# Two matmuls on a zero tile left out of each group of four recurrence steps, in a transformer-like tower on one core

## Chip, cores and metric

The kernel runs on one core of a Trainium2 chip. The metric is the time of one execution on the device, in microseconds (us); the figure compared is the median of several runs. A difference of about 0.3% can be told from no change.

## What is computed

The input is 8 sequences of 512 positions with 128 features. An attention block makes h; a second block, which is where the change lies, adds to h two recurrences over the 512 positions with their readouts; a last block comes down to a layer norm added to h. Of the reference, what matters here:

```python
def res_step(prev, xt):                      # 512 times, one after another
    new = jnp.tanh(xt + prev @ W_res.T)
    new = LEAK * new + (1.0 - LEAK) * prev   # state: 8 x 256
    return (new, new)
def ssm_step(prev, ab_bb):                   # diagonal, elementwise
    ab, bb = ab_bb
    h = ab * prev + bb
    return (h, h)
def readout(s):
    return gelu(_ln(s, ro_g, ro_b) @ W_ro.T + b_ro)
return reservoir_out * gate + ssm_out * (1.0 - gate)   # two readouts, blended
```

## The kernel before

Five engines work from instruction streams of their own, in program order, and wait for each other by semaphores. PE is TensorE (PEld its weight loads), ACT ScalarE, DVE VectorE, POOL GpSimd.

**The recurrence** has 512 steps in 32 bodies of 16 (`STEPS`). Its state stands in PSUM as 128x16 (2 halves of 256 features, 8 sequences). One step is: PE waits for the rounded state `y16` and issues 8 products with the high and low weights (L1323), one for the kept part (`kp16`, L1330), 4 with the low part of the state (`y_lo`, L1323), and one for the low kept part (`kp_lo`, L1335), whose end lets ACT go on. ACT makes `y16` by a tanh (L560), the same in f32 into `ys` (L561), and `kp16` (L563). DVE makes `y_lo` (L949, from `ys` and `y16`) and `kp_lo` (L952). So the steps form one chain through PE, ACT and DVE, and every engine gets other work in between, written out by hand behind each step.

**Beside the recurrence** the bodies 0 to 23 hold the attention of later tiles. Bodies 24 and 25 hold the preparation of the second recurrence. From body 26 (`FIRST_READ`) on, the readouts of tiles 0 to 23 run, one tile (128 positions of one sequence) in each group of four steps, u = t % 4, spread by `body_readouts`. The rest of the 32 tiles' readouts run behind the recurrence in `rest_of_readouts`, with `alone=True`, about 617 us to the end.

What a group holds behind the scan of each step, with n the new tile:

- PE: `feed` (L1506, two f32 passes of 128 columns) in u = 0 and u = 2; the reads `read_one` (L1521, two f32 passes of 258 columns): tile n - 1's last piece in u = 0, tile n's first in u = 1, second in u = 2, third in u = 3. Ahead of the reads of u = 1 and u = 3 stands `keep_clock` (L1236), one product of the identity with the tile `ballast`, which is all zeros, 512 columns of f16, into the bank that the read then starts afresh. The read of u = 1 waits for `readout_scaled`, which DVE's L1102 of u = 0 gives; with the ballast that wait stands ahead of the ballast.
- ACT: sum of squares (L641) in u = 0 and u = 1, gelu (L630) in u = 2, a mean (L634) and the output's norm (L623) in u = 3.
- DVE: the second recurrence (L1127) in u = 0 and 2, its input (L1118) in u = 1 and 3, the readout's scaling (L1102) in u = 3 and u = 0, statistics (L1157, L1160) in u = 1, and a sum over a sequence (L1000) in some steps.
- POOL: in u = 2 a variance and its root (L453 waits for L641 of u = 1; L456), then the layer norm's numbers (L464, L466, L469, L470); in u = 3 difference and base of the blend (L477, L478); in the next u = 0 the blend (L442, L446).

The scan's queue order on each engine is: scan of step t, then the step's other work.

Of the kernel before, what the change touches and what calls it, by code (L numbers as in the profile page):

```python
# [59 lines left out]
def build(nc, x, w_wall, w_mats, w_rows, out):  # L60
    ctx = ExitStack()
    with ctx:
# [122 lines left out]
        PS = ctx.enter_context(nc.psum_tensor("PS", [P, 8, 512], F32))  # L185
# [141 lines left out]
        def read_banks(n, e):  # L327
            if isinstance(n, int) and n >= IN_SCAN:
                return (2 + 2 * ((n + 2) % 4)) % 8
            return 2 + 2 * e  # L330
# [872 lines left out]
        def _(pe):  # L1203
# [31 lines left out]
            def keep_clock(bank, size=512):  # L1235
                t_.matmul(bank[:, 0:size], ident16[:, :], ballast[:, 0:size], start=True, stop=True, skip_group_check=True)  # L1236
# [280 lines left out]
            def read_one(r, m, j, e):  # L1517
                bank = PS[:, read_banks(j, e) + r, 0:3 * (P + 1)].rearrange("p (g n) -> p g n", n=P + 1)
                dst = bank[:, 0:3:2, :] if m == 0 else bank[:, 1:3, :]
                src = ys[:, m * B + j % B, 1 + (j // B) * P:1 + (j // B) * P + P] if r == 0 else ssm[:, m, j // B + 1, (j % B) * P:(j % B) * P + P]  # L1520
                t_.matmul(dst, src, ro_pair[:, m, :].rearrange("p (g n) -> p g n", n=P + 1),  # L1521
                          start=m == 0, stop=m == NH - 1, skip_group_check=True).then_inc(read_piece, 1)

            def readout(u, n, e, active, fed, kept_bodies, alone=False):
                if 1 in active and u == 0:
                    read_one(1, 1, n - 1, 1 - e)
                if 0 in active and u == 1:
                    pe.wait_ge(sigma_ready, NH * n + NH + ROWS_FREE)
                    if alone and n == IN_SCAN:
                        pe.wait_ge(ssm_scaled, NT * NH)  # L1530
                    elif alone and n == IN_SCAN + 1:
                        pe.wait_ge(kp_lo_ready, L + 1)
                    else:
                        pe.wait_ge(readout_scaled, n - (3 if alone else 1) + TWO_FREE)
                    keep_clock(PS[:, read_banks(n, e), :])
                    read_one(0, 0, n, e)
                if 0 in active and u == 2:
                    read_one(0, 1, n, e)
                if 0 in active and u == 3:
                    pe.wait_ge(ssm_done, fed + EIGHT_FREE)  # L1540
                    keep_clock(PS[:, read_banks(n, e) + 1, :])
                    read_one(1, 0, n, e)

            pe.wait_ge(pv_done, NA * NT)
# [25 lines left out]
            for i in range(FIRST_READ, BODIES):  # L1570
                for t in range(STEPS):
                    scan_body(t, i, i % REGIONS)
                    if t % 2 == 0:
                        feed(t // 2, i - FIRST_DECAY)
                    body_readouts(readout, t, i)
            rest_of_readouts(readout)


# [39 lines left out]
```

## Time and profile before

| | |
|---|---|
| median of 3 runs | 648.57 us (648.22 to 649.84) |
| profiled execution | 652.12 us |
| its span, first to last instruction | 650.3 us |
| mean granted TensorE clock | 0.983 of 2.4 GHz |
| PE busy | 610.5 us (94%) |
| DVE busy | 551.8 us (85%) |
| ACT busy | 457.5 us (70%) |
| POOL busy | 188.1 us (29%) |
| ballast products, L1236 (this helper, whole kernel) | 162, 50.4 us busy |

The profile shows one execution, with the start and length of each instruction, and for idle time of an engine what ended it. Ends of matmuls are modelled, since they are pipelined: starts are what to read on PE. A group of a view is named by the source line; the line of a helper stands for all that call it. Times are from the start of the span.

### The profile page before, as it was taken

What the parts mean: (1) busy time and instruction counts of PE and PEld (TensorE: products, weight loads), DVE (VectorE), ACT (ScalarE), POOL (GpSimd) and SP (SyncE); (2) the same over time, 40 slices, a digit from 0 to 9 for tenths busy, and PEclk for the clock granted to TensorE, in tenths of its full rate; (3) what the DMA queues carried; (4) which work ended last, traced back from release to release, by engine and by line L of the source; (5) the groups of instructions that cost most, each with busy time, mean ns of one, the idle gap of its engine ahead of it and who ended that gap; (6) DMA issues with size and microseconds to landing.
All of it is one profiled execution on the core that took longest, in us unless ns stands there. A gap on an engine that the chain in (4) does not pass through costs nothing.

```text
span 650.3 us, 28178 instructions
## 1 busy us (share of the span) xinstructions
PE 610.5 (94%) x11048; PEld 482.0 (74%) x11048; DVE 551.8 (85%) x2298; ACT 457.5 (70%) x2243; POOL 188.1 (29%) x411
## 2 busy tenths in 40 slices
PE   7888877999999999999999999999999999999974
PEld 2554444788888888888888888888888788888852
DVE  5799997788888889898998999899657688999986
ACT  4696876577777777777776777677565566667775
POOL 1554454000000000000000000010000088888887
PEclk9999997999999999999999999999999899999998
DMA  6000000000000000000000000000000000000001
GB/s 206 2 2 1 2 1 2 4 3 4 4 3 4 4 3 4 4 4 4 4 4 3 4 3 4 4 4 3 4 3 4 2 11 15 19 15 19 15 26 29
DMA packets 6325, 7.25 MB, mean 11 GB/s; under 512 B 688, under 2 KB 4784, under 8 KB 6192
## 3 DMA queue, kind: packets, MB, share of 16 engines
q1 hardware_dynamic: 5904, 4.46, 2.2%
q8 instruction: 87, 1.43, 1.0%
q10 hardware_dynamic: 288, 0.99, 0.5%
q14 instruction: 46, 0.38, 0.2%
HBM read 3.35 MB, written 2.10 MB: 8 GB/s over the span
## 4 chain that ended last, share of the span: by engine, by line
PE 64%; POOL 18%; issue 7%; DVE 5%; ACT 4%; DMA 1%; POOLq 0%; SPq 0%
PE PS L1323 25%; PE PS L1377 14%; PE PS L1335 4%; POOL r_dev L456 4%; POOL ln_small L466 3%; PE PS L1341 3%; PE PS L1272 2%; PE PS L1273 2%; PE PS L1279 2%; PE PS L1213 2%; PE PS L1330 2%; PE PS L1247 2%; POOL h_all L446 2%; PE PS L1236 2%; POOL ln_small L470 1%
## 5 line engine op out<-in xcount | busy, mean ns | idle before, releaser
L560 ACT ACTIVATE y<-PS 128x16 f16<-128x16 f32 x512 | 94.3, 184 | 145.1 <-PE PS L1335 143.7
L1377 PE MATMUL PS<-ballast,ident 128*128 128x220 f16 (+5 forms) x722 | 150.3, 283 | 0.0
L949 DVE TENSOR_TENSOR y_lo<-ys,y 128x16 f16<-128x16 f32 x512 | 98.4, 192 | 60.2 <-ACT ys L561 54.7
L1323 PEld LDWEIGHTS PS<-y,res_hi 128*128 128x128 f16 x2048 | 96.2, 96 | 56.0 <-ACT y L560 21.4
L1323 PE MATMUL PS<-y,res_hi 128*128 128x8 f16 x2048 | 128.8, 169 | 0.4 <-ACT y L560 0.3
L1323 PE MATMUL PS<-y_lo,res_hi 128*128 128x8 f16 x2048 | 128.3, 168 | 0.2
L1323 PE MATMUL PS<-y,res_lo 128*128 128x8 f16 x2048 | 123.4, 166 | 0.0
L952 DVE SCALAR_TENSOR_TENSOR kp_lo<-PS,setup,kp 128x16 f16<-128x16 f32 x512 | 115.1, 225 | 0.0
L395 POOL TENSOR_TENSOR small<-small,minus_half 128x2 f32<-128x2 f32 x32 | 22.5, 704 | 318.2 <-DVE y_lo L949 283.6
L522 ACT ACTIVATE prob<-PS,exp_up,sc 128x512 f32<-128x512 f32 x128 | 100.4, 790 | 2.1 <-PE PS L1259 2.1
L527 ACT ACTIVATE prob_hi<-PS,exp_up,sc 128x512 f16<-128x512 f32 x128 | 100.6, 792 | 0.0
L561 ACT ACTIVATE ys<-PS 128x16 f32<-128x16 f32 x512 | 99.0, 193 | 0.0
L563 ACT ACTIVATE kp<-PS 128x16 f16<-128x16 f32 x512 | 97.3, 190 | 0.0
L1335 PE MATMUL PS<-kp_lo,carry_id 128*128 128x16 f16 x512 | 91.9, 179 | 0.0
L831 DVE TENSOR_REDUCE top<-PS 128x1 f32<-128x512 f32 x128 | 86.7, 681 | 3.7 <-PE PS L1247 3.4
L1323 PEld LDWEIGHTS PS<-y_lo,res_hi 128*128 128x128 f16 x2048 | 85.6, 96 | 5.3 <-DVE y_lo L949 0.4
L1323 PEld LDWEIGHTS PS<-y,res_lo 128*128 128x128 f16 x2048 | 87.2, 96 | 0.0
L1330 PE MATMUL PS<-kp,carry_id 128*128 128x16 f16 x512 | 86.5, 169 | 0.0
L863 DVE TENSOR_TENSOR prob_lo<-prob,prob_hi 128x512 f16<-128x512 f32 x96 | 65.3, 682 | 0.2 <-issue 0.2
L1236 PE MATMUL PS<-ballast,ident 128*128 128x512 f16 (+1 forms) x162 | 50.4, 377 | 9.5 <-DVE ys L1000 5.0
L1377 PEld LDWEIGHTS PS<-ballast,ident 128*128 128x128 f16 x722 | 56.5, 97 | 0.2
L1335 PEld LDWEIGHTS PS<-kp_lo,carry_id 128*128 128x128 f16 x512 | 48.9, 95 | 0.0
(207 smaller groups left out, 1336.8 us busy)
## 6 DMA issues: line engine op xcount, KB each, us to landing
ys<-in_x SPq DMA_DIRECT2D x8, 256.0 KB, 8.4
out<-gate_all SPq DMA_DIRECT2D x32, 64.0 KB, 1.5
mats<-in_mats ACTq DMA_DIRECT2D x1, 709.0 KB, 5.1
rows<-in_rows ACTq DMA_DIRECT2D x1, 257.5 KB, 8.0
wall<-in_wall SPq DMA_DIRECT2D x1, 256.0 KB, 4.9
```

What stands on the lines that cost most here:

```text
L522: a_.activation(prob[:, a, :], X[a], ACT.Exp, scale=e_col[:, j % B:j % B + 1], bias=exp_up[:, :])
L527: a_.activation(prob_hi[:, a, :], X[a], ACT.Exp, scale=e_col[:, j % B:j % B + 1], bias=exp_up[:, :]).then_inc(prob_ready, 1)
L560: a_.activation(y16[:, :].rearrange("p (m b) -> p m b", m=NH), pre, ACT.Tanh, scale=back).then_inc(y16_ready, 1)
L561: a_.activation(ys[:, :, bass.ds(i * STEPS + (1 + t), 1)].rearrange("p (m b) o -> p m (b o)", m=NH), pre, ACT.Tanh, scale=back).then_inc(a ...
L563: a_.activation(kp16[:, :].rearrange("p (m b) -> p m b", m=NH), pre, ACT.Copy, scale=keep_scale).then_inc(kp_ready, 1)
L831: v.reduce_max(top[:, a:a + 1], X[a], AX_X).then_inc(top_ready, 1)
L949: v.tensor_tensor(y_lo[:, :], ys[:, :, bass.ds(i * STEPS + (1 + t), 1)].rearrange("p n o -> p (n o)"), y16[:, :], ALU.subtract).then_inc(l ...
L952: v.scalar_tensor_tensor(kp_lo[:, :].rearrange("p (m b) -> p m b", m=NH), PRE[t % 2][:, r, :, t // 2, :], setup[:, 24:25], kp16[:, :].rear ...
L1323: t_.matmul(dst[:, m, :], wts[:, k, m * P:m * P + P], st[:, k * B:k * B + B], start=False, stop=False, skip_group_check=True)
L1330: t_.matmul(dst, carry_id[:, :], kp16[:, :].rearrange("p (m b) -> p m b", m=NH), start=False, stop=False, skip_group_check=True)
L1335: t_.matmul(dst, carry_id[:, :], kp_lo[:, :].rearrange("p (m b) -> p m b", m=NH), start=False, stop=True, skip_group_check=True).then_inc( ...
L1377: t_.matmul(at[:, 0:size], ident16[:, :], ballast[:, 0:size], start=False, stop=True, skip_group_check=True)
```

## The change

In the readouts beside the recurrence the ballast product ahead of the read is no longer issued, in u = 1 and in u = 3. Behind the recurrence (`alone`) both stay. The waits stay where they are, now directly ahead of the read.

```diff
                     else:
                         pe.wait_ge(readout_scaled, n - (3 if alone else 1) + TWO_FREE)
-                    keep_clock(PS[:, read_banks(n, e), :])
+                    if alone:
+                        keep_clock(PS[:, read_banks(n, e), :])
                     read_one(0, 0, n, e)
                 if 0 in active and u == 2:
                     read_one(0, 1, n, e)
                 if 0 in active and u == 3:
                     pe.wait_ge(ssm_done, fed + EIGHT_FREE)
-                    keep_clock(PS[:, read_banks(n, e) + 1, :])
+                    if alone:
+                        keep_clock(PS[:, read_banks(n, e) + 1, :])
                     read_one(1, 0, n, e)
```

## Rows read from the trace of the kernel before

**Rows 1.** By stretches: length, busy us (count) of PE, PEld, DVE, ACT, POOL; clock, DMA.

```profile
479.00:488.00 9.00, 9.00 (x183) 8.88 (x181) 3.62 (x21) 8.35 (x39) 0.00 (x0) 1.00 0.01 2
501.00:509.00 8.00, 7.46 (x120) 5.81 (x121) 5.93 (x27) 3.65 (x25) 0.00 (x0) 1.00 0.01 2
509.50:512.80 3.30, 3.30 (x36) 2.57 (x35) 1.65 (x8) 0.73 (x7) 0.00 (x0) 0.55 0.02 5
515.00:617.00 102.00, 100.14 (x1592) 84.38 (x1591) 92.34 (x383) 69.63 (x447) 84.40 (x212) 1.00 0.06 15
```

**Rows 2.** The same, of instructions on the ballast tile alone: PE, PEld, DVE; clock, DMA.

```profile
479.00:488.00 9.00, 0.00 (x0) 0.00 (x0) 0.00 (x0) 1.00 0.01 2
501.00:509.00 8.00, 2.54 (x7) 0.70 (x7) 0.00 (x0) 1.00 0.01 2
...
515.00:617.00 102.00, 16.94 (x45) 4.32 (x45) 0.00 (x0) 1.00 0.06 15
```

**Rows 3.** Waits, 515 to 617 us: who waited for whom, us, times, longest.

```profile
POOL r_var L453 <- ACT k L641: 56.2, 22, 45.9
```

**Rows 4.** Chain that ended last, 583 to 593 us: start, length, what.

```profile
583.93 0.19 POOL r_var L453
...
587.66 0.07 issue
...
588.18 0.14 issue
...
592.60 0.27 issue
```

**Rows 5.** Timeline of ACT, 582.8 to 592 us: start, length, engine, line, operation.

```profile
582.85 0.18 ACT L560 ACTIVATE y<-PS 128x16 f16<-128x16 f32 x1 [0.31 <-PE PS L1335]
...
585.17 0.18 ACT L560 ACTIVATE y<-PS 128x16 f16<-128x16 f32 x1 [0.46 <-PE PS L1335]
...
586.18 0.18 ACT L560 ACTIVATE y<-PS 128x16 f16<-128x16 f32 x1 [0.23 <-PE PS L1335]
...
587.28 0.18 ACT L560 ACTIVATE y<-PS 128x16 f16<-128x16 f32 x1 [0.31 <-PE PS L1335]
...
588.63 0.18 ACT L560 ACTIVATE y<-PS 128x16 f16<-128x16 f32 x1 [0.36 <-PE PS L1335]
...
591.83 0.18 ACT L560 ACTIVATE y<-PS 128x16 f16<-128x16 f32 x1 [0.31 <-PE PS L1335]
```

**Rows 6.** Timeline of all engines around the ballast of one u = 3.

```profile
584.97 0.17 PE L1335 MATMUL PS<-kp_lo,carry_id 128*128 128x16 f16 x1
...
584.99 0.38 PE L1236 MATMUL PS<-ballast,ident 128*128 128x512 f16 x1
...
585.21 0.60 PE L1521 MATMUL PS<-ro_pair,keep 128*128 128x258 f32 x2
...
585.58 0.23 DVE L952 SCALAR_TENSOR_TENSOR kp_lo<-PS,setup,kp 128x16 f16<-128x16 f32 x1
585.64 0.24 PE L1323 MATMUL PS<-y,res_hi 128*128 128x8 f16 x4
...
585.97 0.17 PE L1335 MATMUL PS<-kp_lo,carry_id 128*128 128x16 f16 x1
...
586.00 0.47 PE L1506 MATMUL PS<-xn,b_t 128*128 128x128 f32 x2
```

**Rows 7.** Timeline of all engines behind u = 1 of the next group.

```profile
587.73 0.45 POOL L446 TENSOR_TENSOR h_all<-k 128x128 f32<-128x128 f32 x1
...
587.85 0.36 DVE L949 TENSOR_TENSOR y_lo<-ys,y 128x16 f16<-128x16 f32 x1
...
588.13 0.22 DVE L952 SCALAR_TENSOR_TENSOR kp_lo<-PS,setup,kp 128x16 f16<-128x16 f32 x1
...
588.41 0.18 PE L1335 MATMUL PS<-kp_lo,carry_id 128*128 128x16 f16 x1
```

**Rows 8.** Source line L446, 500 to 617 us: ns min/median/max, first and last start.

```profile
L446 POOL TENSOR_TENSOR h_all<-k x21: 453/456/621, 522.2 to 614.7; 128x128 f32<-128x128 f32 x21
```

## Prediction, made before the changed kernel was seen

> **What bounds the kernel now.** I read the busy table by stretches first. The readouts beside the recurrence run from about 515 to 617 us. There PE is busy 100.1 of 102 us, DVE 92.3, POOL 84.4, ACT 69.6 [rows 1]. That suggests PE as the bound, and the change takes work from PE. But a busy PE says nothing about which wait ends last, so I went to the waits, the chain and single groups. In the chain that ended last, the stretch around 583 to 593 us lies almost wholly on POOL: its ten operations follow each other with 0.07 us at most between two (587.66), and its only rest is ahead of L453, 0.14 us of issue at 588.18 and 0.27 at 592.60 [rows 4], where it waits for ACT's sum of squares L641 (22 such waits between 515 and 617 us [rows 3], of which the first is its idle time before the readouts). So each group of four steps is a ring: ACT's L641 in step u = 1, POOL's chain from L453 to L446, and from there back to the recurrence. The way back is seen in step u = 1 of a group: POOL's L446 runs 587.73 to 588.18, DVE's L949, started at 587.85, ends only at 588.21, 0.03 behind L446, L952 ends at 588.13 + 0.22 = 588.35 and the last product of the scan, L1335, starts 0.06 later at 588.41 [rows 7]. It waited for DVE, and DVE for POOL. The next step's ACT L560 starts at 588.63 [rows 5].
>
> **What is taken away, on PE.** Bodies 26 to 31 have 24 groups of four steps, and each loses two products of 128x512: one in u = 1, one in u = 3; 48 in all, of which 45 fall between 515 and 617 us [rows 2]. One costs PE: with the ballast between, the read starts 0.24 us after the last product of the scan (584.97 to 585.21); an f32 product straight behind the scan starts after 0.03 (585.97 to 586.00) [rows 6]. That is 0.20 us each, 9.6 us of PE time. Nothing is added, no wait goes or moves: the waits ahead of the ballast now stand ahead of the read. The rest is which of this reaches the end.
>
> **The ballast of u = 3.** Ballast at 584.99, read at 585.21, next scan's first product at 585.64, its last at 585.97 [rows 6]. PE is last here: DVE's L952 ended at 585.58 + 0.23 = 585.81. Without the ballast PE would start the scan at 585.44 and could end it 0.33 later, at 585.77; but the last product can't start before L952's end plus the 0.06 of above, 585.86. So the step gets 585.97 - 585.86 = 0.11 us shorter, not 0.20: the rest goes into a wait for DVE. 24 x 0.11 = 2.6 us.
>
> **The ballast of u = 1.** Where POOL holds L949, it is hidden altogether: 588.41 is L952's end plus 0.06, whatever PE does [rows 7]. It costs something only in groups that POOL doesn't hold. L446 runs for the first time at 522.2 us [rows 8], so the first three groups are free of it, and three or four more are where fills make PE late (those behind the turn of a body, and in the one body with fills at t = 4, 5, 8, 9). I take 0.2 for half of these and 0.11 for the others: about 1.0 us in all. If nothing were given back, the change would bring 2.6 + 1.0 = 3.6 us, some 4.0 with products at half clock at 509.5 to 512.8 [rows 1].
>
> **What is given back.** Now the ring. Call T the time from L560 of u = 1 to L560 of u = 1 in the next group, and a the length of the first step behind it. In the rows, u = 1 starts at 582.85, 587.28 and 591.83, so T is 4.43 and then 4.55; a of the second is 588.63 - 587.28 = 1.35 and its other three steps take 591.83 - 588.63 = 3.20; with the same three steps the first group's a is 4.43 - 3.20 = 1.23 [rows 5]. The groups of the last two bodies repeat this pair. POOL's L446 ends a fixed time after the L560 at which its chain began: 588.18 - 582.85 = 5.33. So the step after it begins at 582.85 + 5.78 = 588.63: T + (next a) = 5.78, as far as POOL holds it. T itself is a plus the other three steps. Two groups together then take 2 x 3.20 + (5.78 - 3.20) = 8.98, the rows' 591.83 - 582.85. The change makes 3.20 into 3.09: two groups take 2 x 3.09 + 2.69 = 8.87, so 0.055 us a group and not 0.11. Half of what u = 3 gives is lost, since the next u = 1 comes earlier and meets the same L446 later in its step. POOL allows that: its chain takes 588.18 - 583.93 = 4.25 (L453 at 583.93), plus 0.07 between two of its operations that depend on each other, is 4.32; T would be 4.43 [rows 4, 7].
>
> **The sum.** 21 groups with POOL's chain at 0.055: 1.2 us. The first three, three times 0.11 and three times about 0.15: 0.8. Groups where fills make PE late: 0.3, less 0.2 given back where POOL's hold begins again: 0.1. Together 2.1 us. The profiled execution took 652.12 us (span 650.3, 1.8 us around it), 3.5 over the median of the runs, of which the half clock near 510 us explains about 1. Profiled I expect 650.0, and the runs' median 648.57 - 2.1 = 646.5 us. The tail behind 617 us keeps its ballasts and its order, and begins when the recurrence and POOL's chain reach it, so it moves as a whole.
>
> **The clock.** Ballast is there for TensorE's clock, so its loss must be priced. The granted clock is 1.00 (2.4 GHz) all through 515 to 617 us, with 16.9 us of ballast in 102; it is also 1.00 from 479 to 488 us, where no ballast runs at all, between the same recurrence's products and f32 products of 128 columns; and it fell to 1.2 GHz at 509.5 us, after a stretch with 7 ballasts (2.5 us) in 8 [rows 1, 2]. So ballast neither is needed everywhere nor suffices everywhere; what is left in the readouts, two f32 passes of 258 columns a step, is more than either of the others has. Price: at half clock PE got through 36 products in 3.3 us, against 1592 in 102, so 52 [rows 1]: 16 products, 1.0 us a stay. The Trainium skill (TensorE: Matmul & The Clock Gate, "What's actually happening") says that the throttled state is the default and that activity releases it. It speaks against this change; the trace shows the fall, but not that these 48 products prevent one here.
>
> **Rivals.** (1) Nothing is given back: POOL's L446 gets out of the way too, or DVE's hold is weaker with another phase. For it: POOL waits for ACT, so it has 0.1 to 0.3 us to spare. Against: the two kinds of group, 0.12 apart, have the same 5.78. It gives 648.57 - 4.0 = 644.6. (2) All is given back: the earlier u = 0 only puts DVE's operations deeper under POOL's, the chain behind L453 gets 0.1 us longer by the lock, as L446's own durations of 453 to 621 ns show [rows 8]. 20 groups x 0.05 (half of 0.1) = 1.0 off the gain, down to 1.1, or all of it at 0.2: 647.5 to 648.6, no change. (3) Slower: the clock falls within the readouts, at first in the groups at 520 to 560. One mechanism, 1.0 us a stay; from two or three stays on it outweighs the 2.1. With one stay in each of six bodies: 646.5 + 6 = 652.5. (4) The title says "left out", and the diff leaves out just this; that the products are still issued I give nothing.
>
> **How the numbers follow.** Forecast, half given back (645.8 to 647.3): 0.50, of which a quarter lies within 0.3%. Nothing given back: 0.13. All or most given back: 0.29. Clock falls, slower: 0.08. The measurement of this kernel tells about 0.3% (1.95 us) from no change, and 2.1 us is hardly past it, so faster 0.50 (0.37 + 0.13), same 0.42, slower 0.08. The range for 8 in 10 reaches from the rival without giving back to no change and a little over: 644.4 to 649.0.
>
> **What would show it.** Right: the step from L560 of u = 3 to that of u = 0 (586.18 - 585.17 = 1.01 [rows 5]) down to 0.90; L1335 there 0.06 behind L952; T of 4.41 to 4.46 in all groups of the last two bodies, no longer 4.43 and 4.55 in turn; T + a still 5.78; the rest of POOL ahead of L453 down by 0.05 on average; PE busy down and more idle of PE put down to DVE's L952 and L949. Wrong: T + a smaller (rival 1) or larger (rival 2), or a granted clock under 1.00 between 515 and 617 us (rival 3).

## The result and the profile after

The changed kernel takes 644.87 us in the median of 6 executions (lowest 644.24), the kernel before 649.75 us in 6 beside them: a ratio of 0.992, with a 95% interval of 0.9892 to 0.9948, so 5 us less. Repeated, with 13 executions against 35, it was 645.52 against 650.5 us, ratio 0.9919 (0.9877 to 0.9961). The time lies in the predicted range of 644.4 to 649.0, but the gain is about two and a half times the 2.1 us of the forecast, and even past the 4.0 us of "nothing is given back". That the time lies in the range is luck: the forecast started from 648.57 us, and the same kernel took 649.75 us in the executions beside this one. A gain of 4.9 us taken from 648.57 would be 643.7, under the range.

The profiled execution of the changed kernel took 662.49 us, one of those in which TensorE stays at half clock for some 50 us in the readouts (5 of this kernel's 19 took 660.6 to 668.1 us); the ratios leave such executions out, the medians don't.

The head of the page of after; the digits are tenths in 40 slices.

```profile
span 660.7 us, 28082 instructions
...
PEclk9999998999999999999999999999998556999998
```

The changed kernel by stretches: length, busy us (count) of PE, PEld, DVE, ACT, POOL; clock, DMA.

```profile
507.10:558.10 51.00, 51.00 (x523) 39.48 (x520) 27.61 (x121) 21.79 (x146) 23.68 (x58) 0.50 0.02 6
559.00:627.00 68.00, 67.83 (x1083) 57.43 (x1083) 62.28 (x276) 49.54 (x315) 60.86 (x154) 1.00 0.07 17
```

Two different kernels stand in this one profile. From 507 to 558 us the clock is 0.50, i.e. 1.2 GHz, and PE is busy in all of it. From 559 us on it is 1.00 again, and this part can be laid beside before's. [rows 1] had POOL busy 84.4 of 102 us, 83%; here it is 60.86 of 68, 89%, and the recurrence goes faster. The waits of POOL say the same. Engine, who it waited for, us in total, times, longest; after, 559 to 618 us:

```profile
POOL r_var L453 <- ACT k L641: 2.7, 1, 2.7
```

Before had 22 such waits between 515 and 617 us [rows 3]; 12 of them, 3.3 us, lie behind 562 us. Here there is one, at the turn to body 28 and ahead of 562 us, and behind it POOL never waits for ACT. Three groups of the changed kernel, by the four starts of ACT's L560 in u = 1 (timeline, start, length, in brackets the idle time before it):

```profile
603.18 0.18 ACT L560 ACTIVATE y<-PS 128x16 f16<-128x16 f32 x1 [0.30 <-PE PS L1335]
...
607.48 0.18 ACT L560 ACTIVATE y<-PS 128x16 f16<-128x16 f32 x1 [0.31 <-PE PS L1335]
...
611.73 0.18 ACT L560 ACTIVATE y<-PS 128x16 f16<-128x16 f32 x1 [0.31 <-PE PS L1335]
...
616.02 0.18 ACT L560 ACTIVATE y<-PS 128x16 f16<-128x16 f32 x1 [0.31 <-PE PS L1335]
```

They take 4.30, 4.25 and 4.29 us, mean 4.28; before's 4.43 and 4.55 [rows 5], mean 4.49. I had allowed 4.43. Both questions of the experiments stand in this one profile: why a group is 0.21 us shorter, and why the clock fell.

Below, groups are numbered from 0 by that L560 of u = 1; 0 to 2 are the first three (L446 runs for the first time at the end of group 2), 3 to 7 the rest up to the turn to body 28, 8 to 22 the full pattern behind it. There the clock was 1.00 in every profile, but for the first 1.1 us of group 8 in after_again and 0.9 us in after_no25. All lengths are differences of such starts.

### The profile page after: what moved, and what is told of

Its sections match the earlier page's. It is cut to its first block, busy times and chain, and to the rows that moved or that the text cites. A ratio compares the mean times of both kernels' runs of the same rounds, so it can differ in the third digit from the quotient of the medians.

```text
span 660.7 us, 28082 instructions
## 1 busy us (share of the span) xinstructions
PE 621.5 (94%) x11000; PEld 489.3 (74%) x11000; DVE 545.7 (83%) x2298; ACT 457.5 (69%) x2243; POOL 189.0 (29%) x411
## 3 DMA queue, kind: packets, MB, share of 16 engines
q1 hardware_dynamic: 5904, 4.46, 2.1%
## 4 chain that ended last, share of the span: by engine, by line
PE 64%; POOL 18%; issue 8%; DVE 5%; ACT 4%; DMA 1%; POOLq 0%; SPq 0%
PE PS L1323 25%; PE PS L1377 14%; PE PS L1335 4%; POOL r_dev L456 3%; POOL ln_small L466 3%; PE PS L1341 2%; PE PS L1272 2%; PE PS L1273 2%; PE PS L1279 2%; PE PS L1213 2%; PE PS L1330 2%; PE PS L1247 2%; POOL k L442 2%; POOL ln_small L470 1%; POOL k L478 1%
## 5 line engine op out<-in xcount | busy, mean ns | idle before, releaser
L560 ACT ACTIVATE y<-PS 128x16 f16<-128x16 f32 x512 | 94.4, 184 | 155.5 <-PE PS L1335 151.5
L949 DVE TENSOR_TENSOR y_lo<-ys,y 128x16 f16<-128x16 f32 x512 | 95.1, 186 | 72.8 <-ACT ys L561 67.8
L1323 PEld LDWEIGHTS PS<-y,res_hi 128*128 128x128 f16 x2048 | 99.5, 98 | 62.5 <-ACT y L560 21.4
L1323 PE MATMUL PS<-y,res_hi 128*128 128x8 f16 x2048 | 130.3, 169 | 0.4 <-ACT y L560 0.3
L952 DVE SCALAR_TENSOR_TENSOR kp_lo<-PS,setup,kp 128x16 f16<-128x16 f32 x512 | 115.2, 225 | 0.0
L1335 PE MATMUL PS<-kp_lo,carry_id 128*128 128x16 f16 x512 | 92.3, 180 | 0.0
L1335 PEld LDWEIGHTS PS<-kp_lo,carry_id 128*128 128x128 f16 x512 | 49.1, 96 | 0.0
L1330 PEld LDWEIGHTS PS<-kp,carry_id 128*128 128x128 f16 x512 | 49.0, 96 | 0.0
```

Of the source, the lines that this page charges most:

```text
L560: a_.activation(y16[:, :].rearrange("p (m b) -> p m b", m=NH), pre, ACT.Tanh, scale=back).then_inc(y16_ready, 1)
L949: v.tensor_tensor(y_lo[:, :], ys[:, :, bass.ds(i * STEPS + (1 + t), 1)].rearrange("p n o -> p (n o)"), y16[:, :], ALU.subtract).then_inc(l ...
L952: v.scalar_tensor_tensor(kp_lo[:, :].rearrange("p (m b) -> p m b", m=NH), PRE[t % 2][:, r, :, t // 2, :], setup[:, 24:25], kp16[:, :].rear ...
L1323: t_.matmul(dst[:, m, :], wts[:, k, m * P:m * P + P], st[:, k * B:k * B + B], start=False, stop=False, skip_group_check=True)
L1330: t_.matmul(dst, carry_id[:, :], kp16[:, :].rearrange("p (m b) -> p m b", m=NH), start=False, stop=False, skip_group_check=True)
L1335: t_.matmul(dst, carry_id[:, :], kp_lo[:, :].rearrange("p (m b) -> p m b", m=NH), start=False, stop=True, skip_group_check=True).then_inc( ...
```

## The experiments

### First round: which ballast, and where the changed kernel's groups stand

**The same kernel again**, on the chip of the other three.

> The changed kernel once more. Its first profile had TensorE at half clock (1.2 GHz) from 507 to 558 us and lasted 662.5 us, while five other executions took 644.2 to 645.4. Theory A (order of DVE and POOL): at full clock the groups of four steps last 4.27 us instead of 4.49, because DVE's L949 now comes ahead of POOL's L477 and L446 and doesn't wait for them; time 5 us under the kernel before. Theory B (as forecast, the hold of POOL stays and half is given back): groups of 4.43, 2.1 us under it. Theory C (clock): how often the clock falls near 507 us decides; an execution in which it falls is 15 to 18 us longer, the others are not.

Measured: 0.9919 as told. Its profile fell into half clock again, from 509.0 to 563.6 us. What came behind was a surprise: its groups 8 to 22 took 67.48 us, as long as before's 67.60, not the 64.44 of the first profile of the same code. Groups 16 to 22, far behind the rise of the clock, say the same: 31.48 us against 31.38 before and 29.96 in the first profile. One such group (ACT, L560 of u = 1, of u = 2, and of the next u = 1):

```profile
603.01 0.18 ACT L560 ACTIVATE y<-PS 128x16 f16<-128x16 f32 x1 [0.40 <-PE PS L1335]
604.37 0.18 ACT L560 ACTIVATE y<-PS 128x16 f16<-128x16 f32 x1 [0.36 <-PE PS L1335]
...
607.47 0.18 ACT L560 ACTIVATE y<-PS 128x16 f16<-128x16 f32 x1 [0.31 <-PE PS L1335]
```

T is 4.46, the step of u = 1 takes 1.36, its idle time 0.36 as before [rows 5]. So the code has two rates at one clock, and what u = 3 gave is given back at the slower one: groups 16 to 22 take 4.50 us each, before's 4.48. Where it goes can be read off the steps. That of u = 3 takes 0.91 us (before 1.00). In one group of two the step of u = 1 takes 1.32 (before 1.23), and in the other that of u = 0 takes 1.20 (before 1.10), since the scan's end now waits for DVE there too:

```profile
611.08 0.46 POOL L477 TENSOR_TENSOR k<-k 128x128 f32<-128x128 f32 x1
611.14 0.43 DVE L949 TENSOR_TENSOR y_lo<-ys,y 128x16 f16<-128x16 f32 x1
...
611.77 0.18 PE L1335 MATMUL PS<-kp_lo,carry_id 128*128 128x16 f16 x1
```

L949 ends 0.03 us behind L477, L952 at 611.50 + 0.22 = 611.72, and L1335 follows 0.05 behind that.

**Only the ballast of u = 3 left out** (the edits from here on are against the changed kernel).

```diff
-                    if alone:
+                    if True:
                         keep_clock(PS[:, read_banks(n, e), :])
```

> Only the ballast of u = 3 is left out in the readouts beside the recurrence, that of u = 1 stays. Theory A: the earlier u = 0 puts L949 ahead of L477, so the order turns with this ballast alone; what then is last in u = 1 is PE with its ballast, so groups of 4.3 to 4.4 us, 2.5 to 4 us under the kernel before. Theory B: 1.3 us under it (24 x 0.055), groups of 4.43.

Measured: 648.66 us, ratio 0.9954 (0.9911 to 0.9998). Its groups 3 to 7 took 23.18 us against 23.41 before; 8 to 22 took 66.71 against 67.60. Its profiled execution, 660.75 us, held two falls of the clock, the second from 515.7 to 525.7 us, all ahead of group 3. It holds both rates in one execution (ACT):

```profile
564.72 0.18 ACT L560 ACTIVATE y<-PS 128x16 f16<-128x16 f32 x1 [0.31 <-PE PS L1335]
...
569.01 0.18 ACT L560 ACTIVATE y<-PS 128x16 f16<-128x16 f32 x1 [0.31 <-PE PS L1335]
...
573.27 0.18 ACT L560 ACTIVATE y<-PS 128x16 f16<-128x16 f32 x1 [0.31 <-PE PS L1335]
...
591.45 0.18 ACT L560 ACTIVATE y<-PS 128x16 f16<-128x16 f32 x1 [0.31 <-PE PS L1335]
...
595.96 0.18 ACT L560 ACTIVATE y<-PS 128x16 f16<-128x16 f32 x1 [0.40 <-PE PS L1335]
...
600.42 0.18 ACT L560 ACTIVATE y<-PS 128x16 f16<-128x16 f32 x1 [0.31 <-PE PS L1335]
```

4.29 and 4.26 us at 565 to 573, with u = 1's ballast present; 4.51 and 4.46 at 591 to 600. The fast rate doesn't need u = 1's ballast gone, but it was lost in group 13, where the fills of body 29 fall.

**Only the ballast of u = 1 left out.**

```diff
-                    if alone:
+                    if True:
                         keep_clock(PS[:, read_banks(n, e) + 1, :])
```

> Only the ballast of u = 1 is left out, that of u = 3 stays. Theories A and B agree: where POOL holds L949 it is hidden, so only the first groups and those with fills gain; 0.5 to 1.0 us under the kernel before, groups of the last two bodies still 4.43 and 4.55 in turn. If instead it is this ballast that turns the order, 3 us or more.

Measured: 649.89 us, ratio 0.9974 (0.9929 to 1.0019), no difference that can be told. Groups 3 to 7: 23.42 us, 8 to 22: 67.27, at the slower rate throughout. Alone it is worth 0.3 us in 15 groups; the step's price of nothing where POOL holds L949 was right.

**Ballast kept in the first two readout bodies (26 and 27), left out from 28 on.**

```diff
-                    if alone:
+                    if alone or n < 8:
                         keep_clock(PS[:, read_banks(n, e), :])
```

(and the same at u = 3)

> Both ballasts stay in the first two bodies of the readouts (8 groups, about 507 to 545 us) and are left out in the last four (16 groups). Theory A: 16 x 0.22 = 3.5 us under the kernel before. Theory B: 0.9 to 1.2. Theory C: if the clock falls near 507 us, it rises again one stay later, as in the kernel before (3.4 us at half clock), since the ballasts are there; no execution 15 us longer.

Measured: 647.52 us, ratio 0.9964 (0.9917 to 1.0011). Profiled at 645.15 us, without a fall of the clock in the readouts: groups 0 to 2 13.00, 3 to 7 23.41 as before, 8 to 22 64.42. So the 15 late groups alone hold 3.0 to 3.2 us of the gain, and they take the fast rate without any change in the first eight. No execution was 15 us longer than the others: the longest took 657.02 us.

### Second round: at an undisturbed clock, and who bounds the fast rate

The clock made the profiles of the first eight groups unreadable. Two ballasts more, ahead of body 26's first step, were to hold it.

**The changed kernel with two ballasts behind body 25.**

```diff
+            for n in range(2):
+                keep_clock(PS[:, 2, :])
             pe.wait_ge(decayed, 2 * 2 * NQ)
             for i in range(FIRST_READ, BODIES):
```

> The changed kernel with two more ballasts of 512 columns behind body 25, in front of body 26, where ACT's table load holds the next step for 1.3 us in any case. Theory C: the clock falls near 507 us because PE does little from 503 to 509 us, and then stays down since the readouts at half clock have too little work without ballast; filled up here, it falls seldom or not at all, no execution of 660 us or more, median 644.5 us like the undisturbed executions of the changed kernel, and the profile shows the first groups at full clock. If the fall has nothing to do with what PE does there: as many long executions as of the changed kernel (5 of 19). Theory A: groups of 4.27 us from the first held group or at least from 545 us on.

**The kernel before with the same two.**

> The kernel before with the same two ballasts added and both ballasts of the readouts kept. Theory C: its long executions (656 to 661 us, 11 of 35) become fewer if they come from this place; the undisturbed ones keep 648 to 650 us, at most 1 us less where the short fall at 509 us is avoided. So the filled changed kernel should be 4 to 5 us under this one.

Measured: 643.6 us, ratio 0.9918 (0.9858 to 0.9978), and 649.33 us, ratio 0.999 (0.9935 to 1.0045). These two share everything but the change, and their profiles hold full clock in all of the readouts. In us:

```
groups                         0-2     3-7     8-22    0-22
before, two ballasts added    13.00   23.40   67.50   103.90
changed, two ballasts added   12.21   22.16   64.52    98.89
```

First and last start of groups 8 to 22, here the changed one's (ACT):

```profile
540.94 0.18 ACT L560 ACTIVATE y<-PS 128x16 f16<-128x16 f32 x1 [0.76 <-PE PS L1335]
...
605.46 0.18 ACT L560 ACTIVATE y<-PS 128x16 f16<-128x16 f32 x1 [0.31 <-PE PS L1335]
```

The first three groups give 0.79 us (I had 0.8), the other twenty 4.22, 0.21 each (I had 0.055). Behind the recurrence 0.3 us is lost again: from the last L560 to the end 33.59 us before, 33.88 now, where POOL's last chain comes later against it; that is where it shows, its cause was not tried. How a group gets to 4.28 us is seen here (filled, timeline of all engines):

```profile
582.02 0.18 ACT L560 ACTIVATE y<-PS 128x16 f16<-128x16 f32 x1 [0.48 <-PE PS L1335]
...
582.42 0.23 DVE L952 SCALAR_TENSOR_TENSOR kp_lo<-PS,setup,kp 128x16 f16<-128x16 f32 x1
...
582.70 0.18 PE L1335 MATMUL PS<-kp_lo,carry_id 128*128 128x16 f16 x1
...
582.92 0.18 ACT L560 ACTIVATE y<-PS 128x16 f16<-128x16 f32 x1
...
583.23 0.18 DVE L949 TENSOR_TENSOR y_lo<-ys,y 128x16 f16<-128x16 f32 x1
583.26 0.46 POOL L477 TENSOR_TENSOR k<-k 128x128 f32<-128x128 f32 x1
...
583.85 0.57 DVE L1127 TENSOR_TENSOR_SCAN keep<-keep 128x128 f32<-128x128 f32 x1
584.02 0.18 ACT L560 ACTIVATE y<-PS 128x16 f16<-128x16 f32 x1 [0.30 <-PE PS L1335]
584.11 0.57 POOL L442 TENSOR_TENSOR k<-k,gate_all 128x128 f32<-128x128 f32 x1
584.35 0.36 DVE L949 TENSOR_TENSOR y_lo<-ys,y 128x16 f16<-128x16 f32 x1
584.63 0.22 DVE L952 SCALAR_TENSOR_TENSOR kp_lo<-PS,setup,kp 128x16 f16<-128x16 f32 x1
584.75 0.46 POOL L446 TENSOR_TENSOR h_all<-k 128x128 f32<-128x128 f32 x1
584.90 0.18 PE L1335 MATMUL PS<-kp_lo,carry_id 128*128 128x16 f16 x1
...
585.16 0.20 POOL L453 TENSOR_TENSOR r_var<-r_ss,r_eps 128x2 f32<-128x2 f32 x1
...
585.24 0.29 DVE L1157 BATCH_NORM_STATS2 ln_st<-h_all 128x6 f32<-128x128 f32 x1 [0.20 <-POOL h_all L446]
...
585.67 0.15 DVE L949 TENSOR_TENSOR y_lo<-ys,y 128x16 f16<-128x16 f32 x1
...
586.02 0.18 PE L1335 MATMUL PS<-kp_lo,carry_id 128*128 128x16 f16 x1
...
589.52 0.20 POOL L453 TENSOR_TENSOR r_var<-r_ss,r_eps 128x2 f32<-128x2 f32 x1
```

Read it against [rows 7]. In u = 0, DVE's L949 starts at 583.23, 0.03 ahead of POOL's L477, and takes 0.18. DVE's scan L1127 starts ahead of POOL's L442, which takes 0.57 and not the 0.45 it takes before. In u = 1, L949 is held by L442, not by L446: it ends at 584.71, 0.03 behind L442's end at 584.68 and ahead of L446's start. Before it ended 0.03 behind L446. L1335 comes 0.88 us after the L560 of u = 1 (584.90 - 584.02), where it came after 1.13 (588.41 - 587.28). L453 follows L446 at once, with no bracket: POOL has no rest. The kernel before, u = 0 of the group in [rows 7]:

```profile
586.37 0.46 POOL L477 TENSOR_TENSOR k<-k 128x128 f32<-128x128 f32 x1
...
586.48 0.37 DVE L949 TENSOR_TENSOR y_lo<-ys,y 128x16 f16<-128x16 f32 x1
```

Here L477 is first, and L949 ends 0.02 behind it. (In every second group of before, L949 of u = 0 starts so late in L477 that this costs it only 0.05 us; L949 of u = 1 is held by L446 in nearly all, in full in the last two bodies.) So there are two orders in which DVE and POOL take turns on what they can't do together, **POOL first** (before) and **DVE first** (after), each repeating itself from group to group. The Trainium skill (SBUF — State Buffer, "Who interferes with whom") says that a VectorE instruction with two SBUF inputs contends with a GpSimd instruction that reads SBUF, that this contention is an exclusive lock, and "Issue order, not op shape, decides who blocks." The trace agrees: the same L949 takes 0.18 where it starts 0.03 us ahead of POOL's, 0.36 and 0.37 where it starts behind, and then ends 0.02 to 0.03 after POOL.

The order also changes the way back from POOL to the recurrence. POOL first, it is the hold of L949 by L446 in u = 1. DVE first, it is a wait by semaphore: DVE's statistics L1157 need the result of L446, and L949 of u = 2 stands behind them in DVE's program. L446 ends at 585.21, L1157 has waited 0.20 us and starts at 585.24, L949 starts at 585.67, L952 ends at 585.97, and L1335 starts at 586.02. Such waits in the filled kernel (545 to 606 us), then in the kernel before (551 to 615 us):

```profile
DVE ln_st L1157 <- POOL h_all L446: 3.3, 14, 0.6
...
DVE ln_st L1157 <- POOL h_all L446: 0.2, 1, 0.2
```

If POOL bounds the DVE-first order, one more operation on POOL must show in full, and one less must help.

**One POOL operation more (0.19 us), off every dependence.**

```diff
+                    if not alone:
+                        g.tensor_tensor(pool_spare[:, 0:1], eps_col[:, :], minus_one[:, :], ALU.add)
```

(behind the L470 of the chain)

> The filled kernel with one more small operation on POOL (128x1, about 0.19 us) in each group beside the recurrence, behind L470. Theory A': POOL is the bound in the fast order, so each group with a chain costs 0.19 more: 20 x 0.19 = 3.8 us over the filled kernel. If the groups were bound by the steps of PE, ACT and DVE, and POOL only met them: under 1 us.

Measured: 646.76 us, ratio 0.9933 (0.9879 to 0.9987), 3 us more than without it. Groups 3 to 7 22.77 us, 8 to 22 66.63, against 22.16 and 64.52: 0.14 us for each operation in the 15 late groups. That is under the 0.19 that I had expected, but the operation moves the next one back by no more than 0.15 us (it starts at 585.30, the next at 585.45), so nearly all of it shows. Its POOL never waits for ACT between 545 and 609 us, and the time appears behind the semaphore of above: the step of u = 2 takes about 1.42 us in all but one of the last seven groups, where it takes 1.11 to 1.13 in the filled kernel, with DVE's statistics waiting for POOL 14 times and 7.2 us. So POOL's chain, from L453 to L453 without a rest (585.16 to 589.52 in the unburdened one, 4.36 and 4.2 in turn), is what the shorter group is made of.

**One POOL operation less: the chain's `ln_var + eps` on DVE.**

```diff
-                    g.tensor_tensor(ln_small[:, s, 0:1], ln_mv[:, s, 1:2], eps_col[:, :], ALU.add).then_inc(ln_var_ready, 1)
...
+                    v.tensor_scalar(ln_small[:, 1 - e, 0:1], ln_mv[:, 1 - e, 1:2], EPS, None, ALU.add).then_inc(ln_var_ready, 1)
```

> The filled kernel with one operation of POOL's chain moved to DVE: the sum of variance and epsilon (L464), for all 32 tiles. Theory A': in the fast order POOL itself is the bound (no rest ahead of L453), so its chain gets 0.28 us shorter (0.21 and the 0.08 behind it) and the groups shorten until PE is last, 4.27 to about 4.15; the tail, where POOL is busy 0.84 of the time, gains up to 12 x 0.25. 3 to 5 us under the filled kernel. If PE or DVE bound the groups: under 1 us, or slower by DVE's 0.1 us a group.

Measured: 644.92 us, ratio 0.9909 (0.9867 to 0.9952), no faster than with the operation on POOL: groups 3 to 7 22.66 and 8 to 22 65.44, 0.9 us longer than 64.52. That was a miss of mine, and tells most. Its rows (line numbers are two lower, L947 is L949):

```profile
603.74 0.46 POOL L476 TENSOR_TENSOR k<-k,h_all 128x128 f32<-128x128 f32 x1
603.80 0.43 DVE L947 TENSOR_TENSOR y_lo<-ys,y 128x16 f16<-128x16 f32 x1
...
604.69 0.59 POOL L446 TENSOR_TENSOR h_all<-k 128x128 f32<-128x128 f32 x1
604.96 0.35 DVE L947 TENSOR_TENSOR y_lo<-ys,y 128x16 f16<-128x16 f32 x1
...
605.73 0.20 POOL L453 TENSOR_TENSOR r_var<-r_ss,r_eps 128x2 f32<-128x2 f32 x1 [0.44 <-ACT k L639]
```

The shorter chain brings POOL's operations forward until they stand ahead of DVE's again: L947 of u = 1 starts behind L446 and ends 0.03 behind it, as in 12 of the groups; here L947 of u = 0 is held too, by L476, and takes 0.43. POOL rests 0.44 us for ACT, 13 times and 4.8 us between 545 and 609 us. DVE has one operation more (0.15 us, in u = 1, behind the statistics), but the step of u = 2, which would show it, takes 1.10 us as in the other kernels; what grew is the step of u = 1, about 1.16 and 1.27 in turn against 1.11 and 1.15. So with less to do POOL meets DVE in the worse order, and here the order matters more than the work. This run no longer tests what bounds the DVE-first order, since the kernel left that order.

### Third round: what the ballast does for the clock, and what u = 1's is worth

**The changed kernel without the ballasts of body 25 too** (one in each of its last 14 steps; the second edit is the same in the kernel before).

```diff
-                if t >= 2:
-                    keep_clock(PS[:, 2, :])
```

> The changed kernel without the 14 ballasts of body 25 too (495 to 507 us). Theory C: with less work for PE there the clock falls in front of the readouts in most executions, and since the readouts have no ballast it stays down until the fills of body 28, some 50 us: 658 us or more, groups of 6.53 us in the first two bodies. If the readouts' reads were enough by themselves to release the clock: down for one or two stays (3 to 7 us), under 650 us.

**The kernel before without them.**

> The kernel before without the 14 ballasts of body 25; the readouts keep theirs. Theory C: the clock falls in front of the readouts as in the sister run, but the ballasts of the readouts release it within one or two stays: 3 to 7 us at half clock behind 509 us, and 8 us or more faster than the sister run where that one falls. If the ballasts of the readouts have no part in it: as long at half clock as the sister.

Measured: 663.32 us, ratio 1.0159 (1.0031 to 1.0286), and 650.07 us, ratio 1.0027 (0.9979 to 1.0075). The clock fell in both profiles at about 496 us. By stretches, first the kernel before, then the changed one:

```profile
496.50:509.00 12.50, 12.11 (x162) 10.55 (x159) 8.48 (x38) 4.64 (x31) 0.00 (x0) 0.50 0.01 2
509.50:560.00 50.50, 49.65 (x793) 41.84 (x791) 42.44 (x179) 33.15 (x219) 36.88 (x92) 1.00 0.04 12
```

```profile
496.50:509.00 12.50, 12.11 (x162) 10.49 (x160) 8.96 (x40) 4.63 (x31) 0.00 (x0) 0.50 0.01 2
509.50:560.00 50.50, 50.50 (x517) 39.35 (x515) 25.91 (x117) 21.91 (x145) 24.16 (x58) 0.50 0.03 7
```

The first stretch is the same in both. Then the readouts begin, with ballast in the one and none in the other: the one is at 2.4 GHz from 509.4 us on, the other stays at 1.2 GHz until 561.3, 3.7 us behind the start of body 28's first fills. So ballast in the readouts doesn't merely keep the clock, it brings it back. The other profiles agree: falls that reached into the readouts lasted 3.4 us (before), 6.8 (u1_only), 10.2 (u3_only) and 13.7 (this one) with ballast there, and 51.2, 54.6 and 64.9 us (after, after_again, after_no25) without. But ballast isn't the only thing that does. In before_filled (the kernel before with two ballasts added) the clock fell at 476.5 us and came back at 496.9. By stretches, of instructions on the ballast tile alone (PE, PEld, DVE; clock, DMA), and the first ballast of body 25:

```profile
477.00:496.50 19.50, 0.00 (x0) 0.00 (x0) 0.00 (x0) 0.50 0.01 2
...
497.00:497.60 0.60, 0.00 (x0) 0.05 (x1) 0.00 (x0) 1.00 0.00 0
...
497.66 0.38 PE L1236 MATMUL PS<-ballast,ident 128*128 128x512 f16 x1
```

Body 24 has no ballast, and the clock was back 0.8 us before the first one of body 25 began; what was new on PE by then were body 25's f32 products L1506, from 494.19 us on. In u3_only it is the same: back at 498.5, first ballast at 499.26. The Trainium skill (TensorE: Matmul & The Clock Gate, "What's actually happening") has the throttled state as the default, released by activity. The pair without body 25's ballasts agrees with that, and so does the rise without ballast, which came with other products on PE; my reading of the trace of before, that products enough were left in the readouts, did not hold.

**The filled kernel with only u = 3's ballast left out.**

> The filled kernel with the ballast of u = 1 kept in the readouts, so only that of u = 3 is left out, now with the clock up. Theory A (two orders of DVE and POOL on their common port): the groups up to body 28 take the fast order as in the filled kernel (4.26 to 4.30 us); at the fills of body 29 PE is late by the ballast and the slow order comes back (4.46 and 4.51) and stays: 9 groups x 0.21 = 1.9 us and 0.6 to 0.9 in the first groups and in body 29, so 2.5 to 3 us over the filled kernel. If the ballast of u = 1 simply costs its 0.2 us wherever PE is last: a rise spread over all groups, no jump at body 29.

Measured: 648.4 us, ratio 0.9963 (0.992 to 1.0007). Groups 0 to 2 12.81, 3 to 7 23.19, 8 to 22 66.76. I had expected 2.5 to 3 us over the filled kernel, and it was 4.8 by the medians (on different chips), 3.9 by the groups of the two profiles, since I had expected the DVE-first order from the start. It was there in groups 8 to 12 alone; groups 3 to 7, and all from body 29's fills on, were POOL first.

**The same, with u = 1's ballast left out in body 29 alone** (groups 12 to 15), where the order had been lost.

```diff
-                    if alone:
+                    if alone or not 12 <= n < 16:
                         keep_clock(PS[:, read_banks(n, e), :])
```

> As the last, but in body 29 alone (4 groups, the body with fills at t = 4, 5, 8, 9) the ballast of u = 1 is left out too. Theory A: the order doesn't turn at body 29, and the last two bodies stay at 4.26 to 4.30 although their ballasts of u = 1 run: within 1 us of the filled kernel. Otherwise no more than 4 x 0.2 = 0.8 us under the run with all ballasts of u = 1, and 4.46 and 4.51 in the last two bodies.

Measured: 645.91 us, ratio 0.9895 (0.9804 to 0.9986). Groups 0 to 2 12.82, 3 to 7 23.19 as in its partner, but 8 to 22 took 64.58 us, not 66.76: the DVE-first order from group 8 to the end. Four ballasts in one body decide over 2.2 us, 1.5 of them in the two bodies behind it (31.46 against 29.99 us for groups 16 to 22), though each is hidden in a steady group. In the others u = 1's ballast cost nothing: 64.58 against the 64.52 of the kernel that has none.

## Why the prediction was right and wrong

**The bound: right in kind.** PE's busy share didn't tell it, the ring of POOL, DVE and ACT did [rows 3, 4].

**u = 3: right.** L952 ends at 582.42 + 0.23 = 582.65 in the filled kernel, L1335 starts at 582.70, and the step takes 582.92 - 582.02 = 0.90, as said; 1.01 before [rows 5]. It is 0.91 in all groups of the POOL-first order, but in the DVE-first order only in every second one; in the others it is 0.98 (586.24 to 587.22).

**u = 1: right as far as it went.** The first three groups gave 0.79 us for both ballasts against 0.8, but the split was off: filled_u3, which keeps that of u = 1, took 12.81 us, so u = 3's gave 0.19 (I had 0.33) and u = 1's 0.60 (I had 0.45). Almost nothing where POOL holds L949 (u1_only, 0.2 to 0.3 us in 15 groups). What was missed is that it decides which order the groups behind the fills fall into.

**"What is given back": the step that failed.** It took T + (next a) = 5.78 as fixed by POOL's chain, since DVE's L949 had always ended behind L446. Measured in the last two bodies, that sum is 5.37 and 5.45 in turn in the filled kernel, where DVE comes first. Even where POOL comes first it didn't stay: 5.78 and 5.88 in turn in after_again, where the hold of L949 by L477 reaches the end of the scan in u = 0 and POOL's chain, L453 to the end of L446, takes 4.36 us instead of 4.25. The sum even held the warning: it let POOL's rest of 0.14 and 0.27 us ahead of L453 [rows 4] shrink, and never asked what happens when the whole of it is gone. In the DVE-first order POOL is in arrears against the recurrence, L477 begins behind L949 of u = 0 and L446 behind L949 of u = 1, and the hold that made a step 1.35 us long falls away; the step takes 1.10 to 1.15. The group is then not 4.43 but POOL's own chain, 4.28 us: 0.21 a group instead of 0.055, over 20 groups 4.2 us instead of 1.1. Rival (1) named this ("POOL's L446 gets out of the way too"), but I priced it at the 0.11 of u = 3, not at the hold of L949, and argued against it from two kinds of group that were both of the same order. Rival (2) is also real: in the POOL-first order with u = 3's ballast gone everything was given back (groups 16 to 22 took 31.48 us in after_again and 31.45 in after_no25, 31.38 in before and 31.32 in before_filled). The same code stood in both orders, so the edit doesn't decide the order alone; the state in which the groups are entered has a part. The sum of 2.1 us lay between two states and is none of them, and the time of 644.87 us fell outside the band of 645.8 to 647.3 that the forecast gave to its own mechanism, next to the 644.6 of rival (1), which had a chance of 0.13.

**The clock.** The price of a stay was of the right size, 1.0 us against 1.4: 13.00 + 23.41 = 36.41 us in groups 0 to 7 of kept_two_bodies, 37.78 in the before with 3.4 us at half clock, so 1.4 us for one stay. The count was wrong: I gave one stay a body, but in the three profiles without ballast in the readouts the fall ended only 2.0 to 4.0 us behind body 28's first fills. At half clock a group takes 6.53 us, here in the changed kernel (ACT):

```profile
526.94 0.18 ACT L560 ACTIVATE y<-PS 128x16 f16<-128x16 f32 x1 [1.06 <-PE PS L1335]
533.47 0.18 ACT L560 ACTIVATE y<-PS 128x16 f16<-128x16 f32 x1 [1.06 <-PE PS L1335]
```

Groups 0 to 7 took 52.85 us there and 34.37 in the filled kernel, 18.5 of the 19.1 us between the two spans (660.7 and 641.6). It meets some executions and spares most, which is why the median shows the gain. The mean shows less of it: 650.1 us over the changed kernel's 19 executions, 652.4 over 41 of the kernel before, 2.3 us. The fall itself is older than the change: before falls at 509.1 us for 3.4 us, most of it in [rows 1]. In the five changed kernels with two ballasts more ahead of body 26 no profile holds a fall between 477 and 635 us, and 29 of their 30 executions are under 652 us. That the two ballasts are the cause is what these counts suggest, and not shown: the falls near 476 us are missing from them too, and those come ahead of the two ballasts. With a median of 643.6 us the filled kernel is the best version of these runs, though its ratio of 0.9918 can't be told from the change's own.

**Left open.** Why some executions lose the clock near 476 or 507 us and others don't. Whether the changed kernel takes the DVE-first order in groups 3 to 7 of all its undisturbed executions; the filled one stands for it. Why the changed kernel went on DVE first in its first profile and POOL first in after_again and after_no25: the clock rose 1.9 us ahead of group 8 in the one and 1.1 and 0.9 us inside it in the others, and whether that decides wasn't tried. Why POOL's L464 takes 0.30 us in after_again (609.50) and 0.21 before (584.88), which is most of what its chain is longer.

## What to carry to other kernels

- Two engines that exclude each other, in a loop that closes through both, can have more than one steady order. A fixed sum such as T + a is valid within one order: ask what an edit does to the margin by which one starts ahead of the other (here 0.03 us), and price the other order too, from its own longest chain.
- An engine with a little rest in each turn is not a reserve that can be spent smoothly; look at what happens when it reaches nothing. Less work on it can be slower, as here with one operation moved to DVE.
- Filler products must be judged by what ends a fall of the clock, not only by whether one begins, and over more than one profile.

## What the runs showed of the hardware

- A TensorE that the profile calls busy (50.50 of 50.50 us, 517 products) stayed at 1.2 GHz all that time, and in a kernel that differs only in ballast the same stretch went at 2.4 GHz with 793 products in 50.5 us. The eight groups there took 6.53 to 6.58 us each but for the last (8.24 us, with the turn of the body), and the clock rose only behind the first fills of body 28. In another kernel the clock came back after 20.5 us without any filler product (before_filled, 476.5 to 496.9 us).
- A DVE operation that starts behind POOL's ends 0.02 to 0.03 us after it (L949: 0.15 to 0.18 alone, 0.34 to 0.43 held), and POOL's stretch as well where DVE is first: L442 from 0.45 to 0.57 us behind the scan L1127.
- Moving one operation of about 0.2 us from POOL to DVE made 15 groups 0.9 us longer; the steps that grew are those in which POOL's operations now stand ahead of DVE's.
